# A gated expert layer in float32: one flat loop over pairs of tiles, with a table word per tile, on ScalarE and VectorE

## The reference

```python
# x: 2 x 2048 x 512; E = 32 experts, K = 8 per token, H = 512, F = 192
x = x + layernorm(linear_attention(layernorm(x)))     # 16 heads, 4 key heads
t = layernorm(x)                                      # 4096 tokens
scores = softmax(t @ wg.T)
weights, idx = top_k(scores, 8); weights /= weights.sum(-1)
xs = t[t_s]                                           # rows sorted by expert
g = ragged_dot(xs, w1, group_sizes)                   # 512 x 192 of each expert
u = ragged_dot(xs, v1, group_sizes)
ys = ragged_dot(silu(g) * u, w2, group_sizes)         # 192 x 512 of each expert
out = zeros.at[t_s].add(ys * w_s)
x = x + layernorm(out)
```

## Time and profile before

| | |
|---|---|
| median of 3 runs | 2549.44 us (2547.16 to 2557.21) |
| profiled execution, own time | 2549.61 us |
| its span, first to last instruction | 2547.9 us |
| mean granted clock of TensorE | 0.952 of 2.4 GHz |
| busy share TensorE / VectorE / ScalarE / GpSimd | 89% / 62% / 51% / 37% |
| the loop over expert tiles | 1216 to 2480 us |

### The profile page before, as it was taken

One profiled execution on the slowest core, in us unless ns is written; L12 is line 12 of the kernel. 1 busy time (PEld: TensorE's weight loads), 2 busy tenths in 40 slices (PEclk: granted clock), 3 DMA queues, 4 the chain that ended last, 5 costly groups with the idle time before them and its releaser, 6 DMA issues.

```text
span 2547.9 us, 69695 instructions
## 1 busy us (share of the span) xinstructions
PE 2263.1 (89%) x11804; PEld 1931.4 (76%) x11805; DVE 1574.4 (62%) x4968; ACT 1305.3 (51%) x2786; POOL 952.4 (37%) x1130
## 2 busy tenths in 40 slices
PE   7999899999989999982898889878999898989990
PEld 5887588888868888871797788767898787977980
DVE  4455567777767777763465656555565555656546
ACT  3343556666656656641455555444555554555443
POOL 1112025555535555555133333323333332333342
PEclk9999999999999999995899999989999998999995
DMA  3334113232333333336688877777786777877778
GB/s 117 94 114 114 58 34 127 106 125 106 129 125 120 120 112 126 108 114 212 158 138 178 173 156 166 166 197 161 149 155 133 179 152 181 140 175 143 135 137 289
DMA packets 164993, 358.13 MB, mean 141 GB/s; under 512 B 21184, under 2 KB 21184, under 8 KB 164800
## 3 DMA queue, kind: packets, MB, share of 16 engines
q0 software_dynamic: 60224, 144.21, 28.5%
q1 hardware_dynamic: 104704, 213.21, 28.1%
HBM read 178.21 MB, written 179.14 MB: 140 GB/s over the span
## 4 chain that ended last, share of the span: by engine, by line
PE 26%; DMA 12%; issue 6%; SPq 5%; DVEq 2%; ACT 1%; DVE 1%; POOL 1%; ACTq 1%; POOLq 0%
DMA BIG<-sorted_rows 9%; PE bank L465 5%; PE bank L466 5%; PE bank L467 5%; PE bank L454 3%; DMA moe_sum<-X,aidx 3%; SPq L329 2%; PE bank L482 1%; PE bank L483 1%; PE bank L484 1%; PE bank L486 1%; PE bank L485 1%; PE bank L475 1%; ACT BIG L598 1%; SPq L348 1%
## 5 line engine op out<-in xcount | busy, mean ns | idle before, releaser
L1479 POOL DMA_INDIRECT moe_sum<-X,aidx x274 | 428.5, 1564 | 868.3 <-issue 504.4
L959 PE MATMUL bank<-WB,XH 128*128 128x512 f32 x1536 | 478.5, 393 | 0.0
L465 PE MATMUL bank<-WB,XL 128*128 x1096 | 405.2, 370 | 8.8 <-issue 2.9
L466 PE MATMUL bank<-WB,XH 128*128 x1096 | 379.0, 346 | 0.0
L467 PE MATMUL bank<-WB,XH 128*128 x1096 | 378.8, 346 | 0.0
L959 PEld LDWEIGHTS bank<-WB,XH 128*128 128x128 f32 x1536 | 290.5, 189 | 60.0 <-issue 0.5
L959 PE MATMUL bank<-WB,XL 128*128 128x512 f32 x768 | 316.2, 412 | 10.7 <-DVE XL L1266 10.7
L959 PE MATMUL bank<-WB,SH 128*128 128x512 f32 x1024 | 319.0, 393 | 0.0
L1545 POOL DMA_INDIRECT sorted_rows<-srow,pos x256 | 266.4, 1041 | 95.4 <-issue 95.4
L736 DVE SCALAR_TENSOR_TENSOR BIG<-BIG,bank x274 | 95.1, 347 | 322.6 <-ACT BIG L535 234.5
L546 ACT ACTIVATE X<-bank (+1 forms) x276 | 165.1, 598 | 240.7 <-POOLq L845 122.4
(11 more groups left out here) (219 smaller groups left out, 4454.9 us busy)
## 6 DMA issues: line engine op xcount, KB each, us to landing
BIG<-sorted_rows SPq DMA_DIRECT2D x278, 274.0 KB
X<-x_in SPq DMA_DIRECT2D x64, 256.0 KB, 2.8
RAW<-w_in SPq DMA_DIRECT2D x16, 768.0 KB
LATE<-w_in SPq DMA_DIRECT2D x16, 768.0 KB
sorted_rows<-BIG SPq DMA_DIRECT2D x33, 274.0 KB, 5.1
moe_sum<-LATE SPq DMA_DIRECT2D x34, 256.0 KB, 3.0
LATE<-x_in SPq DMA_DIRECT2D x32, 256.0 KB, 3.1
RAW<-wo_in SPq DMA_DIRECT2D x16, 512.0 KB, 3.4
```

The source lines that it names most:

```text
L465: nc.tensor.matmul(eu[s][:, 0:UP], XL[:, s, k, :], wh, start=k == 0, stop=False)
L466: nc.tensor.matmul(eu[s][:, 0:UP], XH[:, s, k, :], wh, start=False, stop=False)
L959: last = nc.tensor.matmul(ps, w, m, start=start and i == 0, stop=stop and i == len(terms) - 1)
L1479: nc.gpsimd.indirect_dma_start(acc_dram[:, :], bass.IndirectOffsetOnAxis(aidx[:, s:s + 1], 0), rows, None, compute_op=ALU.add).then_inc(s_ ...
```

## The change

ScalarE and VectorE now run the same flat loop over pairs of tiles as TensorE. VectorE builds, in some 16 more small operations on one partition, a table with one word per tile: the expert (5 bits), the first piece to convert in this tile and the one after the last (3 bits each), and how many pieces are converted once this tile is through. In each tile both engines read the word and run a short loop over the pieces that it names. The piece's addresses are worked out from the expert's number; for that the two raw buffers became one. The conversion has moved inside the tile: ahead of `rows_high` on ScalarE, and ahead of the tail copy and `rows_low` on VectorE. All pieces take the form with a scale from a tile. Marks are gone. TensorE no longer waits for converted weights, and SyncE loads the next weights once the last ones are there and `rows_low` of a later tile is through. Tiles of the last two experts convert as well, to sets that nobody reads.

```diff
         def load_weights(eng, e, i):
...
-                eng.dma_start(part, src.rearrange("a p n -> p (a n)")).then_inc(s_ewr[i], 16)
+                eng.dma_start(part, src.rearrange("a p n -> p (a n)")).then_inc(s_ewr, 16)
+        def unit_word(eng, g):
+            word = eng.value_load(unit_at[0:1, bass.ds(g, 1)], min_val=0, max_val=2048 * 512 - 1)
+            return word & (EXPERTS - 1), (word >> 5) & 7, (word >> 8) & 7, word >> 11
+
+        def raw_piece(e, k):
+            return RAWS[:, bass.ds((e & 1) * RAW_N + k * PIECE, PIECE)]
+
+        def high_at(e, k):
+            return (e & (WSETS - 1)) * WSET + k * PIECE
...
# SyncE, per expert
-                    sp.wait_ge(s_elo, e + 2)
+                    sp.wait_ge(s_ewr, (e + 3) * 64)
+                    stand(sp)
+                    sp.wait_ge(s_exl, first + 3)
                     stand(sp)
                     load_weights(sp, e + 3, (q + 1) % 2)
...
# TensorE
-            def up(g, s, e, off):
-                pe.wait_ge(s_elo, e + 1)
-                stand(pe)
+            def up(g, s, off):
...
# ScalarE
+            def weights_high(e, k):
+                nc.scalar.activation(WB[:, bass.ds(high_at(e, k), PIECE)], raw_piece(e, k), ACT.Copy,
+                                     scale=sign[:, bass.ds(k >> 2, 1)]).then_inc(s_eh, 1)
...
-                    silu(g, same)
-                    act_high(g - 1, other)
-                    evacuate(g - 2, same)
-                    rows_high(g + 2, same)
-                    if converts(e):
-                        act.wait_ge(s_ewr[i], (e - i) * 32 + 128)
-                        weights_high(to, i, (k & (LOW_PIECES - 1)) * PIECE).then_inc(s_eh, 1)
+            with act.Fori(0, pairs) as p:
+                for s in range(2):
+                    g = 2 * p + s
+                    e, u0, u1, _ = unit_word(act, g)
+                    silu(g, s)
+                    act_high(g - 1, 1 - s)
+                    evacuate(g - 2, s)
+                    act.wait_ge(s_ewr, e * 64 + 192)
+                    stand(act)
+                    with act.Fori(u0, u1) as k:
+                        weights_high(e + 2, nc.s_assert_within(k, 0, PIECES - 1))
+                    rows_high(g + 2, s)
...
# VectorE, the table
+            done(nc.vector.tensor_tensor(first_row, tile_no, bank[7][0:1, 0:MAX_TILES], ALU.subtract))
+            done(nc.vector.memset(unit_f, 0.0))
+            settled()
...
+            done(nc.vector.tensor_tensor_scan(wide[1], unit_f, first_row, 0.0, ALU.add, ALU.add))
+            done(nc.vector.scalar_tensor_tensor(wide[0], tile_no, 256.0, wide[0], ALU.mult, ALU.add))
+            settled()
+            nc.vector.scalar_tensor_tensor(unit_at, wide[1], 2048.0, wide[0], ALU.mult, ALU.add).then_inc(s_units, 1)
...
# VectorE, the loop
-                    gate(g, same, e)
-                    act_low(g - 1, other)
-                    add_index(g - 2, same)
-                    rows_low(g + 2, same)
-                    if converts(e):
-                        dve.wait_ge(s_eh, g + (2 * PIECES + 1))
-                        weights_low(to, i, (k & (LOW_PIECES - 1)) * PIECE)
+            with dve.Fori(0, pairs) as p:
+                for s in range(2):
+                    g = 2 * p + s
+                    e, u0, u1, highs = unit_word(dve, g)
+                    gate(g, s, e)
+                    act_low(g - 1, 1 - s)
+                    add_index(g - 2, s)
+                    dve.wait_ge(s_eh, highs + 2 * PIECES)
                     stand(dve)
-                    with dve.Fori(m, PIECES) as k:
-                        low_or_both(to, i, k)
-                    all_low(e + 2)
+                    with dve.Fori(u0, u1) as k:
+                        weights_low(e + 2, nc.s_assert_within(k, 0, PIECES - 1))
+                    tails(g + 2, s)
+                    rows_low(g + 2, s)
```

More of the change, by code:

```diff
@@ L306, in one @@
             def one(e, q, lo):
-                word = eng.value_load(table[0:1, row, bass.ds(e, 1)], min_val=512 + 32768, max_val=8 * 32768 - 1)
-                first, n, m = word & 511, (word >> 9) & 63, word >> 15
-                body(e, q, first, n, m, lo)
+                word = eng.value_load(table[0:1, row, bass.ds(e, 1)], min_val=512, max_val=64 * 512 - 1)
+                first, n = word & 511, word >> 9
+                body(e, q, first, n, lo)
                 return first + n
@@ L382, in moe_sp, with body @@
                 sp.sem_inc(s_fill[i], 16)
-            def body(e, q, first, n, m, lo):
+            def body(e, q, first, n, lo):
                 i = q % 2
@@ L491, in experts_at @@
                 now, before = word & (EXPERTS - 1), word >> 6
-                return now, (now & (WSETS - 1)) * WSET, (before & (WSETS - 1)) * WSET
+                return (now & (WSETS - 1)) * WSET, (before & (WSETS - 1)) * WSET
             pe.wait_ge(s_ld, 16)
@@ L503, in moe_pe @@
                     g = 2 * p + s
-                    e, now, before = experts_at(g)
+                    now, before = experts_at(g)
                     rows_t(g + 1, 1 - s)
-                    up(g, s, e, now)
+                    up(g, s, now)
                     act_t(g - 1, 1 - s)
@@ L553, in moe_act @@
             for e in range(2):
-                act.wait_ge(s_ewr[e], 64)
-                for piece in range(PIECES):
-                    weights_high(e, e, piece * PIECE, sign[:, piece >> 2:(piece >> 2) + 1]).then_inc(s_eh, 1)
-                all_high(e)
+                act.wait_ge(s_ewr, 64 * e + 64)
+                for k in range(PIECES):
+                    weights_high(e, k)
             act.wait_ge(s_T, 3)
@@ L671, in moe_dve @@
             settled()
-            done(nc.vector.scalar_tensor_tensor(tn[0:1, 0, :], tn[0:1, 2, :], 512.0, tn[0:1, 3, :], ALU.mult, ALU.add))
-            done(nc.vector.tensor_scalar(words, tn[0:1, 2, :], float(LOW_PIECES), 32768.0, ALU.min, ALU.mult))
-            settled()
-            nc.vector.tensor_tensor(table[:, 0, :], words, tn[0:1, 0, :], ALU.add)
+            nc.vector.scalar_tensor_tensor(table[:, 0, :], tn[0:1, 2, :], 512.0, tn[0:1, 3, :], ALU.mult, ALU.add)
             nc.vector.tensor_copy(pair_n[:, :], odd[0:1, 2:3]).then_inc(s_tabd, 1)
@@ L721, in tail_at, with tails @@
                 return ((g + RING) & (RING - 1)) * TAIL
-            def rows_low(g, parity):
+            def tails(g, parity):
                 dve.wait_ge(s_T, g + 3)
@@ L726, in rows_low @@
                 nc.vector.tensor_copy(BIG[:, bass.ds(tail_at(g) + WR, TAIL)], BIG[:, at(XR + W_COL, parity, ROW, TAIL)]).then_inc(s_wr, 1)
+            def rows_low(g, parity):
                 dve.wait_ge(s_exh, g + 1)
```

108 lines of the change are left out of this document (50 added, 58 removed).

## The result

The changed kernel takes 2739.91 us (median of 4 runs, 2733.94 to 2740.84); the kernel before took 2548.30 in the same series. The ratio is 1.0739, with a 95% interval of 1.0710 to 1.0769. The predicted time was 2690 us; 2739.91 lies inside the range.

The account below looks back on a forecast made before the run. TensorE (3.9 us a tile) and VectorE's instruction stream (3.85) were taken to bound the loop. 274 x 4.6 + 28 x 5 = 1400 against 1264 us, +136, table +5: +141 on 2549.4, giving 2690 us, range 2600 to 2840.

Parts of the forecast that it names:

- No room on VectorE: Loop over expert tiles, kernel before: VectorE's instruction stream needs 3.85 us a tile, TensorE 3.9, despite VectorE's 62% busy share.
- The tile at 4.6 us: Each of 274 tiles: added and dropped stream rows sum to +0.75 on VectorE's 3.85 us; bounds 4.3 and 5.1.
- the ring of both pieces: Not forecast: two-tile chain of evacuation, ScalarE's piece, VectorE's piece, rows_low and TensorE's tile; measured 9.00 us, 4.50 each.
- asks after ScalarE is done: VectorE's wait for ScalarE's converted piece: piece ready at 4.9 us, VectorE asking at 6.0, so no added wait.
- the series rival: Inside each tile: ScalarE's and VectorE's conversion pieces run in series, 5.1 us a tile, 2830 us; chance 0.17.
- The changes of expert: 28 places: 5 us each (3 to 7) instead of 7.0; slow clock and extra pieces, 2.8 us, mostly hidden.
- The stall's own working: TensorE's wait for rows at a change of expert: weights leave about 2.7 us later; stall 4.8 us late, before 4.2.
- the clock rival: TensorE idles 0.7 us a tile and its clock falls; a third of tiles at 1.2 GHz, 2910 us; chance 0.06.
- SyncE's new waits at nothing: SyncE's waits for landed weights and rows_low at a new expert: both events past by then, priced at nothing.
- The table, +5 (0 to 7): Some 16 small operations before the first conversion of expert 1: 6 us, part hidden, so +5 us.
- A hidden stream: Loop over tiles: VectorE's register work hidden, tile stays at 3.9 us, only savings remain, 2500 us; chance 0.12.
- Savings and stream that cancel near 4.1 us: Loop over tiles: added rows cost half their price in the trace, tile near 4.1 us, 2550 us; chance 0.05.

Follow-up runs that it names:

- b_dve_word: The kernel before, with VectorE also loading a word per tile from the existing table of tiles and taking the gate's expert from it: 2656.21 us, ratio 1.0425.

## Why the prediction was right, and where it wasn't

**No room on VectorE: right.** b_dve_word shows it at the predicted price: +0.66 us a tile for a load priced at 0.7.

**The tile at 4.6 us: right in size (4.52), only half right in cause.** The sum for VectorE's stream, 3.85 + 0.75, was high by some 0.3: opened, the stream takes 4.27, which is the prediction's own lower bound (4.3, with each row that falls out at 0.14 us). Its count was not what erred: the traces have 32 stream rows a tile in the 20 tiles before and 37 or 34 after, 3.5 more, where it had 3 more. What holds 4.52 is the ring of both pieces. The failing step is that VectorE "asks after ScalarE is done", with a microsecond of lead. It put the end of ScalarE's piece at 4.9 us behind the end of a `rows_low`, and VectorE's demand at 6.0. In the tile shown above, counted from 1935.07 (the end of the `rows_low` one tile earlier), VectorE's stream comes to the wait at 6.0, as forecast, but the piece ends at 6.05: TensorE's groups ended at 4.1 and not at 3.5, and ScalarE's stream, of which the prediction said that it goes ahead of its operations and costs nothing, put 0.60 us between evacuation and piece. In 233 of 274 tiles ScalarE was last. That the tile came out so near 4.6 is luck: a stream priced 0.3 us too high met a ring that the sum didn't have. By the letter of the prediction's own test ("VectorE's conversion is released by ScalarE in most tiles") the series rival holds, at a price of 4.5 us. Its 5.1 added 0.5 us to a stream of 4.6; the ring runs through TensorE's tiles and is a length of its own, so nothing adds.

**The changes of expert: the mis-sized term.** Forecast 5 us each (3 to 7) in place of 7.0, measured 7.3 in place of 6.8, so above the range: +13 us and not -56. These 69 us, less 23 by which the tile was forecast too long, plus 3 for the table, make the 49 that the forecast lacks. The stall's own working nearly held. SyncE issued the weights at 1887.28, 3.7 us into the tile; the transposes of one tile stood at 1878.68, those three tiles later at 1896.43:

```profile
1878.68 0.42 PEld L468 LDWEIGHTS bank<-ident,BIG 128*128 128x128 f32 x4 [0.80 <-DMA BIG<-sorted_rows]
...
1896.43 0.72 PEld L468 LDWEIGHTS bank<-ident,BIG 128*128 128x128 f32 x4 [5.03 <-DMA BIG<-sorted_rows]
1896.44 1.12 PE L468 MATMUL bank<-ident,BIG 128*128 128x128 f32 x4 [4.60 <-DMA BIG<-sorted_rows]
```

The weights left 8.6 us after the first of these (forecast 5.3 + 2.7 = 8.0), the rows were there 9.2 us later (forecast 10.5). 17.75 us less three tiles of 4.52 is 4.2 us late, forecast 4.8. What failed is that the rest, 2.8 us, "mostly disappears under the longer tile". TensorE's matmuls stand for 4.60 us here (2.74 in the earlier trace rows); it had been busy 4.67 of the 9.4 us up to 1896.40. Behind it the granted clock was 0.63 over 6.6 us, part of it at 1.2 GHz: the transposes took 1.12 us in place of 0.66, and the next two tiles 5.8 and 5.1 us. Behind the stall of the kernel before, from 1914 to 1920, it was 1.00. Over the loop the clock is 0.94, before 0.96. So a small piece of the clock rival came true at the changes, not inside the experts, where it is 1.00. How the rest of 7.3 divides between this, the leftover pieces inside short experts and the 30 us of late weights there stays open.

**SyncE's new waits at nothing: right.** The row load ahead of the weights was issued at 1883.30; the expert's word and the padding rows fill the time to 1887.28, and both waits were over when SyncE came to them.

**The table, +5 (0 to 7): 8.0 measured.** What the profile should show came as told: inside a long expert TensorE has a gap in each tile, 0.48 us ahead of the up group (forecast 0.7) and 0.30 ahead of the transposes, and a load of 0.3 us stands in each of 274 tiles. Conversions aren't one per tile: ScalarE has 317 in the loop (327 with the ten ahead of it), since short experts take several in one tile.

**The other rivals.** A hidden stream would have given 2500, and b_dve_word alone speaks against it: a load that had room would have cost nothing. Savings and stream that cancel near 4.1 us are ruled out by the 4.52. The Trainium skill's rule (Perfetto Trace Analysis, Per-instruction lifecycle) that a VectorE instruction goes to a wait queue and frees the sequencer agrees with part of the rows: the load of the next tile's word starts at 1943.47, while `rows_low` runs from 1943.40 to 1944.09. On ScalarE the rows differ from it, and the rows decide: none starts while the evacuation waits (last section). It is no reason to price stream rows at zero.

## What to carry to other kernels

Before work is added to a loop, measure the engine's own instruction stream per round, not its busy share: at 62% busy VectorE had no room for one register load. A wait that is a stream row of its own holds all address arithmetic behind it, so it should stand behind that arithmetic, or where what follows isn't needed soon (neither was tried here). A conversion step that a third engine's next tile depends on is best started before the evacuation of the last one: that swap took 54 to 60 us off. A prefetch whose consumer stands inside the tile stalls all engines when it is late: spreading the weights over three tiles gained 27 us with the conversion at the tile's end, and lost 32 or more with it inside.

## What the runs showed of the hardware

ScalarE's stream does not pass an ACTIVATE that still waits for its semaphore. The evacuation (L556) waited from 1938.51 to 1939.19; the next stream rows, those of L581, start only with it, 0.007 us behind its start. It is so in all 265 tiles of the loop in which this evacuation was idle before for over 0.3 us: the next row never starts earlier than 0.005 us behind it. The rows up to the piece then take 1.19 us, half of it beneath the evacuation and 0.60 beyond its end. The register load costs VectorE 0.311 us in the median of 274 tiles and ScalarE 0.282, as the views by line of the changed kernel show:

```profile
L331 DVEq TENSOR_LOAD <-XN x274: 299/311/1000, 1226.7 to 2666.5; - x137
```

```profile
L331 ACTq TENSOR_LOAD <-XN x274: 272/282/1096, 1225.9 to 2663.9; - x137
```

A fused register row isn't one price either: those of the piece's address took 0.276 and 0.179 us where the leftover loop's median was 0.093.
